# A routed feed-forward block around a linear-attention block: indirect transfers spaced by a small memset, and one reciprocal square root per routing group

## What is computed

```
x = x + 0.5 * ffn(layernorm(x))
x = x + att(layernorm(x))
x = x + 0.5 * ffn(layernorm(x))
```

## Time and profile before

| | us |
|---|---|
| median of 3 runs (lowest, highest) | 708.64 (707.14, 710.11) |
| the profiled execution | 711.44 |
| its span, first to last instruction | 709.6 |
| busy: TensorE, VectorE, ScalarE, GpSimd | 546.9, 408.2, 317.3, 256.7 |

### The profile page before, as it was taken

The page is one execution under the profiler, slowest core; times in us unless marked ns, Lnnn a source line. Parts: engine busy times, 40 slices in busy tenths (PEclk is TensorE's granted clock), DMA queues, the critical chain, the costliest instruction groups (busy, mean ns, idle before and its releaser), DMA issues.

```text
span 709.6 us, 16562 instructions
## 1 busy us (share of the span) xinstructions
PE 546.9 (77%) x5242; PEld 480.9 (68%) x5242; DVE 408.2 (58%) x1193; ACT 317.3 (45%) x709; POOL 256.7 (36%) x267
## 2 busy tenths in 40 slices
PE   2128698879889889987677877978898897998920
PEld 2126587768678778776566667857787787997820
DVE  4836866223669885986646677957874423333402
ACT  5325363334384567552455364446652342443400
POOL 1360445455500620015356045056215544044334
PEclk9999899999999999999899789999998999999975
DMA  8933233433221221112111212112212223223212
GB/s 293 327 113 87 79 95 111 127 111 96 66 61 39 64 58 53 47 34 64 53 55 47 79 53 68 42 53 65 87 50 67 84 75 98 78 70 86 62 56 67
DMA packets 88046, 58.91 MB, mean 83 GB/s; under 512 B 10272, under 2 KB 81696, under 8 KB 87968
## 3 DMA queue, kind: packets, MB, share of 16 engines
q1 hardware_dynamic: 54288, 29.44, 14.2%
q0 software_dynamic: 8192, 16.79, 8.4%
q10 hardware_dynamic: 25488, 11.61, 5.6%
HBM read 28.65 MB, written 29.16 MB: 81 GB/s over the span
## 4 chain that ended last, share of the span: by engine, by line
PE 47%; issue 13%; ACT 12%; DVE 11%; another core or an unknown queue 10%; SPq 4%; DMA 1%; POOL 1%; ACTq 0%; POOLq 0%; DVEq 0%
PE py L1105 17%; PE pa L1092 11%; PE pb L1092 10%; ACT xn L735 3%; PE pT L1080 3%; DVE h L976 2%; PE bkB L1144 2%; ACT rT L697 2%; ACT sil L717 2%; ACT yrow L702 1%; DVE xres L986 1%; SPq L577 1%; SPq L564 1%; ACT L780 1%
## 5 line engine op out<-in xcount | busy, mean ns | idle before, releaser
L976 DVE TENSOR_TENSOR h<-sil,pb 128x512 f32<-128x512 f32 x177 | 121.1, 686 | 217.3 <-ACT sil L717 125.4
L1105 PE MATMUL py<-ffn_w,h 128*128 x1416 | 201.5, 286 | 47.8 <-ACT yrow L702 41.2
L660 POOL DMA_INDIRECT yg<-rows_out,slot x128 | 124.1, 970 | 280.7 <-DVE h L976 192.8
L1105 PEld LDWEIGHTS py<-ffn_w,h 128*128 128x128 f32 x1416 | 179.2, 198 | 60.1 <-issue 37.6
L646 POOL DMA_INDIRECT rows_in<-parts,slot x128 | 130.8, 1022 | 164.5 <-DVE h L976 106.0
L1092 PE MATMUL pa<-rT,ffn_w 128*128 128x128 f16 (+1 forms) x1440 | 158.8, 253 | 30.5 <-ACT rT L697 16.8
L1092 PE MATMUL pb<-rT,ffn_w 128*128 128x128 f16 (+1 forms) x1440 | 160.4, 251 | 1.5 <-issue 1.3
L1092 PEld LDWEIGHTS pa<-rT,ffn_w 128*128 x1440 | 118.0, 101 | 55.1 <-issue 39.4
L1092 PEld LDWEIGHTS pb<-rT,ffn_w 128*128 x1440 | 118.0, 101 | 13.3 <-issue 2.0
L717 ACT ACTIVATE sil<-pa 128x512 f32<-128x512 f32 x177 | 105.4, 596 | 27.7 <-PE pa L1092 18.9
L697 ACT ACTIVATE rT<-pT 128x512 f16<-128x512 f16 (+1 forms) x120 | 58.1, 484 | 119.2 <-PE pT L1080 71.3
(11 more groups left out here) (122 smaller groups left out, 416.5 us busy)
## 6 DMA issues: line engine op xcount, KB each, us to landing
rows_out<-yrow ACTq DMA_DIRECT2D x177, 64.0 KB
rin<-rows_in SPq DMA_DIRECT2D x57, 128.0 KB
shared<-in_w SPq DMA_DIRECT2D x16, 256.0 KB, 6.8
rin<-rows_in SPq DMA_DIRECT2D x63, 64.0 KB
rows_in<-zrow SPq DMA_DIRECT2D x30, 128.0 KB
rows_in<-zrow SPq DMA_DIRECT2D x2, 1472.0 KB, 11.1
xres<-in_x SPq DMA_DIRECT2D x4, 512.0 KB, 5.5
ffn_w<-in_w SPq DMA_DIRECT2D x8, 256.0 KB
```

The lines of the kernel that those rows point to most:

```text
L660: pool.indirect_dma_start(yg[:, b, c, j, :], None, rows_out[SET[run]][0:STEPS[run] * T, :], bass.IndirectOffsetOnAxis(ap=slot[:, c, at:at ...
L976: dve.tensor_tensor(h[:, t % RING, :], sil[:, t % 2, :], pb[t % 2][:], ALU.mult).then_inc(s_h, 1)
L1105: mm = pe.matmul(py[:], h[:, (FIRST_STEP[q] + c // per) % RING, at:at + T], w, start=(c == 0), stop=(c == FC - 1))
```

## The change

Two things are changed. Behind each transfer of the planned list, GpSimd clears a 64-byte wide buffer `pace` and counts this up in a semaphore of its own, and it waits for this count before it issues the next transfer of the list. In the plan, and in the kernel, a run's `rsqrt` step is done once, at the place of its last sequence, for all its sequences; the `norm` of each of them waits for it. The planner runs again with this rule, so the places of other steps can move too.

```diff
+PACE = 64
...
+    def scale_of(c):
+
+        return next(o for o in chains if o.steps is NORM and (o.run, o.unit) == (c.run, UNITS[c.run] - 1))
+
     def ready(c):
...
+        if step == "norm":
+            times.append(scale_of(c).ends.get("rsqrt"))
...
         step = c.next()
         eng = ENGINE[step]
+        if step == "rsqrt" and c is not scale_of(c):
+            c.ends[step] = at
+            return
         free[eng] = c.ends[step] = max(free[eng], at) + WORK[eng][step]
         plan.append((tile, step, c.run, c.unit))
...
+        pace = sb("pace", [P, PACE], U8)
...
+        s_pace = sem("transfer_spaced")
...
             for one in every(0, range(UNITS[0])):
                 scatter(*one)
-            for gate, name, *one in TRANSFERS:
+            for sent, (gate, name, *one) in enumerate(TRANSFERS):
                 wait(pool, s_h, gate)
+                wait(pool, s_pace, sent)
                 if name == "scatter":
                     scatter(*one)
                 else:
                     gather(*one)
+                pool.memset(pace[:], 0).then_inc(s_pace, 1)
             for one in every(RUNS - 1, range(UNITS[-1])):
                 gather(*one)
...
-                act.wait_ge(s_rstd, count(RSQRTS, (scale, run, 0 if (scale, run < 2) == ("rsqrt", True) else b)))
+                scaled = b if name == "mnorm" else 0 if run < 2 else UNITS[run] - 1
+                act.wait_ge(s_rstd, count(RSQRTS, (scale, run, scaled)))
...
-                    rsqrt(slice(u, u + (UNITS[run] if name == "rsqrt" and run < 2 else 1)))
+                    rsqrt(slice(U0[run], U0[run] + UNITS[run]) if name == "rsqrt" else slice(u, u + 1))
```

## The result

The changed kernel takes 713.69 us (median of 15 runs, 712.52 to 715.16), the kernel before 708.64 us (702.74 to 714.87) beside it: ratio 1.0087, 95% interval 1.0062 to 1.0111. It is slower by 0.9%. The forecast was 679 us and the range 654 to 713: the time lies 0.7 us above the range, and the change went the other way.

What follows compares the result with a forecast made beforehand. It took TensorE, held up beside close GpSimd transfer sequences, to bound the kernel. From 711.44 us, -30 (spacing), -2 (merged chain) and +2 (GpSimd lateness) gave 681.4, less 2.8 for the median: 679 us, range 654 to 713.

Steps and rivals of the forecast that it cites:

- What bounds the kernel: ScalarE's "remote" waits for late TensorE completions hold 40 us excess, going with close GpSimd transfer sequences; 71 us of chain unattributed.
- What the spacing returns: Spacing GpSimd's planned transfers removes three quarters of the 40 us excess waits: -30 us, from 0 to -56.
- The interval: Time between starts of GpSimd's spaced transfers: 1.6 us, bounds 1.25 and 2.08, against 1.25 to 1.27 before.
- The lateness of GpSimd: Slower issue on GpSimd mostly uses its 192.8 us waiting for tiles ahead of gathers: +2 us, from 0 to +9.
- The merged chain: One square root chain per routing group takes seven chains off VectorE: -2 us, from 0 to -15.
- The later norms of runs 4 and 5: Norms, splits and copies behind the last add, 7 us of ScalarE, covered by slack: nothing, thinly in run 5.
- run 6: Routing group within the kernel, not a measurement; its scatters were claimed done 20 tiles before its start.
- The sum: Whole kernel: -30 - 2 + 2 = -30 us from 711.44, then 2.8 less for the median: 679 us.
- Rival 2: GpSimd becomes the bound at run 4's start, interval above 1.9 us, TensorE still stuck: 717 us (721 or 714), chance 0.12.
- Rival 1: Spacing does not reach the cause of TensorE's stalls; only -2 us left: 706.6 us, 702 to 712, chance 0.18.
- signs named for "right": Transfers 1.5 to 1.7 us apart, remote waits under 15 us, unknown share under 4%, clock above 0.95, chain's last line x15.
- The warnings for the size: Size is wrong if VectorE's h waits for combines before gathers land, or waits move to run 4's transposes.

## Why the prediction was wrong

**What bounds the kernel: right for its job.** 40 us were read off as excess, 71 us as the chain's share, and the kernel before without the remote waits is 708.64 - 630.66 = 78 us shorter: above both. That the loss goes with GpSimd's sequences was right in that spacing took it away entirely, and incomplete: it needs a condition of the job besides. What that condition is stays open: in both, the kernel before has the same instructions, and its transfers start 1.25 us apart.

**What the spacing returns: under-sized.** The step took three quarters of 40, -30 us, because other engines would be late next. With 1.89 us behind each transfer there is no remote wait left, and the changed kernel takes 713.69 us where the kernel before takes 708 and 712.37 where it takes 631: of the 78 us that the remote waits cost the kernel before, it pays 1. With long waits gone, tiles ran faster until the next late transfer.

**The interval: mis-sized.** It was put at 1.25 + 0.12 + 0.25 = 1.6 us and measured 1.89. The error is the wait on GpSimd's own memset, taken as 0.25 from the earlier trace rows and measured as 0.60; the memset itself, taken as 0.12, adds 0.03. The bounds 1.25 and 2.08 held. How much hangs on it shows every second transfer, a mean of 1.57 us, in a job with the remote waits: 664.88 us against 708.77, 44 us faster. So near the interval that the prediction took, if in another pattern, the change goes the way that was forecast, and beyond the 30 us of it.

**The lateness of GpSimd: the step that failed.** It was costed at +2 us, up to +9, by the argument that GpSimd has 192.8 us of idle time ahead of gathers. But that idle time was spent behind gates, and the gates were late because TensorE was. The unchanged kernel without the remote waits shows half of it gone:

```profile
POOL yg L660 <- DVE h L976: 97.1, 41, 32.8
```

Its waits for stores to `rows_out` are longer there (102.6 against 45.5 us), but in all its idle time falls from 709.6 - 256.7 = 453 to 629.9 - 255.1 = 375 us. Where there are no remote waits, the merged kernel pays 712.37 - 625.77 = 87 us for the spacing at 1.89 us, and 648.31 - 625.77 = 23 us at a mean of 1.57: even there, +2 was ten times too low. It is paid at the places that the prediction named, combines and run starts; but it priced eight transfers ahead of one combine as 8 x 0.35 = 3 us, where GpSimd's lateness had piled up over all transfers since its queue last stood idle. From 75.64 us to the first gather at 157.34 it never did: 43 scatters, each 0.63 us longer than at 1.26, are 27 us by this estimate. The first gather may start when 28 h are made; 35 were.

**The merged chain: right alone, -2 forecast.** Its last line ran 15 times as forecast, and alone it gives 625.77 against 630.91, -5 us. The later norms of runs 4 and 5 cost nothing visible there. That run 6's scatters are done 20 tiles before its start was misread: their gates end at 144 and the run begins at 154, 10 tiles; nothing hung on it. Beside the spacing the merged kernel is not faster: 712.37 against 708.48 for the spacing alone, in two jobs whose kernel before agrees within 0.3 us. That its later slots feed a queue that is already late fits this, but was only argued.

**The sum.** 708.64 - 78 (remote waits) - 5 (merged chain) + 87 (lateness of GpSimd) = 712.6, against 713.69 measured. The terms come from jobs without the remote waits, so this is a way to read the runs, and its closeness only says that the changed kernel takes nearly the same time in both conditions. Two large terms of opposite sign nearly cancel, where the prediction had -30 and +2. The lower end of its range, 654, leaves out the -2 of the merged chain; this changes nothing.

**Rival 2** was the case that came: its place, run 4's start, and the side were right. Its condition was not. It wanted GpSimd's interval above 1.9 us with TensorE still stuck; what came was TensorE free and an interval of 1.89. The bound was set against tiles that still ran at the old pace, and the larger part of the waits is at combines, 84.2 us against 51.5 at run starts. That its 714 is near the measured time is luck. Rival 1 did not come about where it was to be tested: there were no remote waits left. Of the signs named for "right", two came in: no remote waits, and the last line x15. Two did not: transfers are 1.89 us apart, not 1.5 to 1.7, and the granted clock at 317 to 400 us is 0.84, not above 0.95, and TensorE waits 25.4 us of that stretch for run 4's first rows. The share of the chain can't be read, because the changed kernel's chain covers only some 7% of the span. The warnings for the size came in both: h waits while gathers land, and waits moved to the transposes of run 4.

## What to carry to other kernels

When a change removes a stall, price the other queues against the pace that the kernel has without the stall, not against the idle time that they show with it: idle time behind gates is borrowed from the stall. An instruction that waits for the one just issued on its own queue costs far more than its work (0.60 against 0.03 us here), so price such a wait by itself before it stands behind each transfer. A planner that is told the measured interval can win a part back (43 us here, with transfers at 1.89 us), and can lose too (14 and 20 us in the two kernels without spacing whose plan moved from 1.5 us to 1.26 and to 1.9). Run the unchanged kernel in several jobs before believing that its stalls are its own: the changed kernel, with spacing at each transfer, is 0.9% slower in one condition and 13% slower in the other, with spacing at every second one it is 6% faster in one and 2.5% slower in the other, and the merged chain alone gains 1% in the one in which it was measured.

## What the runs showed of the hardware

- One kernel had two times, 631 us in five jobs and 708 us in three (the result's among them), each within 2% inside a job, and on one chip both. In the trace of the result's job, ScalarE and VectorE wait 40 times for results of TensorE whose end the profile can't put down to an instruction, 109 us in all and up to 6.3 us at a time, mostly behind close sequences of indirect transfers by GpSimd; with such sequences in the trace of a 631 us job, never. The granted clock from 317 to 400 us was 0.88 against 0.93. What makes a job the one or the other is not known.
- GpSimd: a 64-byte memset behind an indirect transfer takes 0.17 us and adds 0.03 to the interval; each further one adds 0.09 (1.29 to 1.38 for two, 1.90 for eight); waiting for it adds 0.60.
- Indirect transfers of 128 rows of 512 bytes by GpSimd follow each other at 1.25 to 1.27 us when nothing holds them.
- A TensorE that waited 25.4 us ran eight down products 1.7 us later in 2.02 us instead of mostly 1.06 to 1.16; the granted clock there was 0.50, the lower of its two levels.
